# A decoder's 16-head attention, stages three and five: mask by TensorE, sums by a ones column, keys spread by ScalarE, other lags

## What is computed

```
q, k, v = y @ Wq.T, y @ Wk.T, y @ Wv.T          # stage five: q = rope(rmsnorm(y)), k = rope(rmsnorm(ctx)), v = ctx
scores  = q @ k.T / 4, causal mask              # per batch of 64 rows and per head
probs   = softmax(scores)
out     = (probs @ v) @ Wo                      # stage three: only through a modulation of rank 16
m       = 0.1 * tanh(out @ A) * (z @ A2)        # stage three; z is the second norm's input
```

## Time and profile before

| | us |
|---|---|
| median of 3 runs (1977.92 to 2044.46) | 1979.12 |
| the profiled execution | 1981.32 |
| its span, first to last instruction | 1979.4 |
| stage two, from its first transfer to the end | 569 to 705 |
| stage three: statistics, turning, preparation | 705 to 733 |
| stage three: attention | 733 to 915 |
| stage five: statistics, keys | 1476 to 1530 |
| stage five: attention | 1530 to 1676 |
| stage six (feed forward of stage five) | 1676 to the end |

### The profile page before, as it was taken

One profiled execution on the slowest core, in us unless ns is written; L12 is line 12 of the kernel. 1 busy time (PEld: TensorE's weight loads), 2 busy tenths in 40 slices (PEclk: granted clock), 3 DMA queues, 4 the chain that ended last, 5 costly groups with the idle time before them and its releaser, 6 DMA issues. The chain is left out here.

```text
span 1979.4 us, 33807 instructions
## 1 busy us (share of the span) xinstructions
PE 1652.8 (84%) x12770; PEld 1274.6 (64%) x12770; DVE 1253.0 (63%) x2049; ACT 812.3 (41%) x1334; POOL 695.5 (35%) x535
## 2 busy tenths in 40 slices
PE   4999999999948856998997869999960666999997
PEld 3888888888836635776885624444430454788886
DVE  6676777677758878982225869898871897311111
ACT  3555555554526642333223355555520332322222
POOL 0212121212125621001222059999940871232332
PEclk9999999999969968998997879999995698899999
DMA  2011111111030020000001000000019000000001
GB/s 93 14 57 55 63 57 48 56 53 61 24 96 2 3 90 1 2 1 1 1 0 31 5 0 1 1 0 1 0 28 267 1 1 0 1 1 1 1 0 42
DMA packets 59033, 57.45 MB, mean 29 GB/s; under 512 B 17536, under 2 KB 53888, under 8 KB 58928
## 3 DMA queue, kind: packets, MB, share of 16 engines
q1 hardware_dynamic: 58928, 56.00, 9.2%
HBM read 41.31 MB, written 14.68 MB: 28 GB/s over the span
## 5 line engine op out<-in xcount | busy, mean ns | idle before, releaser
L1277 DVE TENSOR_TENSOR s6f_hid<-s6f_act_sb,s6f_u_ps 128x512 f32<-128x512 f32 x64 | 44.0, 687 | 219.1 <-PE s6f_u_ps L1228 219.1
L544 POOL TENSOR_TENSOR s_w_parts<-s_w_raw,s_w_parts 128x768 fp32r<-128x768 f32 x16 | 29.6, 1850 | 429.0 <-ACT s_w_parts L496 429.0
L1300 POOL TENSOR_TENSOR s6f_hid_parts<-s6f_hid,s6f_hid_parts 128x512 fp32r<-128x512 f32 x64 | 82.6, 1291 | 244.3 <-ACT s6f_hid_parts L1266 244.3
L1758 POOL TENSOR_TENSOR s4b_pcs<-s4b_cs,s_p_rows 128x1024 f32<-128x1024 f32 x64 | 120.4, 1903 | 96.6 <-ACT s4b_cs L1804 96.6
L1769 POOL TENSOR_TENSOR s4b_with_re<-s4b_with_re,s4b_with_im 128x1024 f32<-128x1024 f32 x64 | 150.5, 2373 | 2.6 <-DVE s4b_with_im L1723 2.6
L1300 POOL TENSOR_TENSOR s3f_hid_parts<-s3f_hid,s3f_hid_parts 128x512 fp32r<-128x512 f32 x32 | 41.3, 1291 | 265.8 <-ACT s3f_hid_parts L1266 265.8
L1844 PE MATMUL s4b_c_ps<-s4b_pcs,const 128*128 128x512 f32 x256 | 122.5, 601 | 0.0
L420 PE MATMUL s_v_ps<-s_wv_parts,s_xnT 128*128 128x256 f32 x768 | 104.2, 286 | 12.0 <-ACT s_v L525 6.4
L479 PE MATMUL s_o_ps<-s_w_parts,s_zT 128*128 128x256 f32 x768 | 110.4, 294 | 4.1 <-DVE x_rows L583 4.1
L420 PEld LDWEIGHTS s_v_ps<-s_wv_parts,s_xnT 128*128 128x128 f32 x768 | 96.7, 191 | 17.6 <-ACT s_v L525 9.7
L1834 PE MATMUL s4b_turns_ps<-s_theta_bd,s_zc 128*128 128x512 f32 x128 | 78.0, 694 | 31.5 <-DVE s4b_frac L1708 30.4
(11 more groups left out here) (294 smaller groups left out, 4127.3 us busy)
## 6 DMA issues: line engine op xcount, KB each, us to landing
stored_weights<-s1q_halves SPq DMA_DIRECT2D x16, 768.0 KB, 3.7
s6w_parts<-stored_weights SPq DMA_DIRECT2D x32, 384.0 KB, 7.9
s1q_packed<-in_codes SPq DMA_DIRECT2D x8, 384.0 KB, 4.4
s1q_scale<-in_scale_rows SPq DMA_DIRECT2D x8, 384.0 KB, 4.9
x_rows<-in_x SPq DMA_DIRECT2D x1, 2048.0 KB, 8.3
s_w_raw<-in_L_attn_W_Q SPq DMA_DIRECT2D x16, 128.0 KB, 2.2
s_w_raw<-in_L_attn_W_K SPq DMA_DIRECT2D x16, 128.0 KB, 2.3
s_w_raw<-in_L_attn_W_O SPq DMA_DIRECT2D x16, 128.0 KB, 2.4
```

Source lines behind the costliest of these rows:

```text
L1277: nc.vector.tensor_tensor(hid[:, f % 2, :], act_sb[:, f % 2, :], u_ps[:, f % 2, :], ALU.mult) \
L1300: nc.gpsimd.tensor_tensor(hid_parts[:, f % 2, 1, :], hid[:, f % 2, :], hid_parts[:, f % 2, 0, :], ALU.subtract).then_inc(low_done, 1)
L1758: last = nc.gpsimd.tensor_tensor(pcs[:, half, n_, :].rearrange("p (k c) -> p k c", k=HK), cs[:, half, n_, :].rearrange("p (k c) -> p k c", ...
```

## The change

1. The mask is a table of 0 and -1e38, added by TensorE: four float32r products of the identity with it open each tile's scores, and the score products accumulate onto them. The minimum is gone.
2. The values get a 17th column of ones, so that the weighing gives the sums too; the pass over the exponentials is gone. In stage five the spread values of all tiles are made once, on GpSimd, in the keys' block.
3. Keys are spread by ScalarE, with a per-row scale, for two tiles at a time in stage three.
4. Stage three projects q and k from the split halves by float32r products, two tiles at once, q in even steps and k in odd ones; v from both halves by float32. The modulation's factor z @ A2 is made for all tiles in the preparation block. The residual is on GpSimd, all tiles ahead of the low parts. The high parts on ScalarE are done one each in steps 1, 3, 5 and 7.
5. Stage five's queries: ScalarE normalises, GpSimd does four operations with prepared tables; repeated keys are made once in the keys' block.
6. The lags: final and finish 5, `turn_att` 4; all steps are written out. The turned output shares the values' bank.
7. `prefetch` of stage six's weights is issued in the attention's block. The context comes in contiguous layouts made on the host (`ctx_values`, `ctx_rows`).

```diff
-                for half in range(2):
-                    sp.dma_start(vrow[half * S:(half + 1) * S, tiles, :, :].rearrange("k t b d -> k (t b) d"),
-                                 ins["ctx_512"].rearrange("b k d -> k b d")[:, 2 * n * CHUNK:2 * (n + 1) * CHUNK, :]) \
-                        .then_inc(loads[n], 16)
+                sp.dma_start(vrow[:, tiles, :, :].rearrange("p t b d -> p (t b d)"),
+                             ins["ctx_values"][:, 2 * n * CHUNK * S:2 * (n + 1) * CHUNK * S]).then_inc(loads[n], 16)
...
+        va_ps = room.ps("va_ps", [P, 512])
+        v_ps, f_rows, aT_ps = va_ps[:, 0:D], va_ps[:, 0:D], va_ps[:, D:2 * D]
...
-        o_ps, f_ps = of_ps[:, 0:D], of_ps[:, D:2 * D]
-
-        def upto(n):
...
+        def steps(eng, parts):
+            run_steps(eng, NT, parts, head=NT + max(lag for _, lag in parts))
...
+        if prefetch:
+            @block.sync
+            def _(sp):
+                prefetch(sp)
...
+            nc.vector.tensor_copy(ident_r[:, :], core.c("ident")).then_inc(masks, 1)
+            nc.vector.tensor_copy(mask_r[:, :], core.c("mask_add")).then_inc(masks, 1)
...
+            def attended(i, rnd, k):
+                dve.wait_ge(o_full, i + 1)
+                wait(dve, aT_full, i - 1)
+                o = o_ps.rearrange("p (h e) -> p h e", e=EO)
+                nc.vector.reciprocal(rs[:, i % 2, :], o[:, :, E]).then_inc(inverted, 1)
+                dve.wait_ge(inverted, i + 1)
+                nc.vector.tensor_tensor(att[:, i % 2, :].rearrange("p (h e) -> p h e", e=E), o[:, :, 0:E],
+                                        rs[:, i % 2, :].unsqueeze(2).to_broadcast([P, H, E]), ALU.mult) \
+                    .then_inc(att_done, 1)
...
+            def shift(i, rnd, k):
+                scores = s_ps[:, :, 0:4 * S].rearrange("p a (h s) -> p a h s", s=S)
+                dve.wait_ge(s_full, i + 1)
+                nc.vector.tensor_reduce(mx[:, :].rearrange("p (a h) -> p a h", a=4), scores, AX_X, ALU.max) \
+                    .then_inc(maxed, 1)
+                dve.wait_ge(maxed, i + 1)
+                wait(dve, exped, i)
+                nc.vector.tensor_tensor(
+                    sc[:, :, :].rearrange("p (a h) s -> p a h s", a=4), scores,
+                    mx[:, :].rearrange("p (a h) -> p a h", a=4).unsqueeze(3).to_broadcast([P, 4, 4, S]),
+                    ALU.subtract).then_inc(shifted, 1)
...
+                wait(dve, o_full, i - 2)
...
+            steps(dve, [(attended, 4), (shift, 2)] + ([(spread_values, 1)] if own else []) + [(finish, 5)])
...
+                nc.gpsimd.memset(vbd[:, :, :, :, :, :], 0.0).then_inc(zeroed, 1)
+                pool.wait_ge(zeroed, 1)
+                nc.gpsimd.tensor_copy(vbd[:, :, :, :, :, E].rearrange("p k b n h -> p (k b n) h"),
+                                      core.c("half2").unsqueeze(1).to_broadcast([P, 6 * PAIRS, 2])) \
+                    .then_inc(zeroed, 1)
+            def residual(i, rnd, k):
+                nc.gpsimd.tensor_scalar(yt[:, i % 2, :], core.x[:, i, :], mv[:, i, 0:1], rstd[:, i:i + 1],
+                                        ALU.subtract, ALU.mult).then_inc(y_done, 1)
+                pool.wait_ge(y_done, 2 * i + 1)
+                nc.gpsimd.tensor_tensor(core.x[:, i, :], core.x[:, i, :], yt[:, i % 2, :], ALU.add) \
+                    .then_inc(y_done, 1)
...
+            steps(pool, [(residual if own else rope, 0)])
...
+            def normalise(i, rnd, k):
+                wait(act, roped, i - 1)
+                nc.scalar.activation(yt[:, i % 2, :], core.x[:, i, :], ACT.Identity, bias=w["shift"][:, i:i + 1],
+                                     scale=factor[:, i:i + 1]).then_inc(normed, 1)
...
+            def k_copy(n, k, at):
+                rows = qk_ps[:, at:at + NC * AT_ONCE * P].rearrange("p (g s) -> p g s", s=S)
+                for h in range(2):
+                    last = nc.scalar.activation(kbd[:, k, :, :, h, :].rearrange("p c b s -> p (c b) s"), rows,
+                                                ACT.Identity, scale=core.c("blk16")[:, h:h + 1])
+                last.then_inc(k_out, 1)
...
+            def weights(i, rnd, k):
+                if i % 2 == 1 and i // 2 < len(beside[0]):
+                    beside[0][i // 2](act)
+            if own:
+                steps(act, [(probT_copy(0), 3), (tanh, 5), (operands, 0), (probT_copy(1), 3), (attT_copy, 4),
+                            (exponent, 2), (weights, 0)])
+            else:
+                steps(act, [(normalise, 0), (probT_copy(0), 3), (operands, 1), (probT_copy(1), 3), (attT_copy, 4),
+                            (exponent, 2)])
...
+                pair = i // 2
+                if i % 2:
+                    pe.wait_ge(q_out, pair + 1)
+                else:
+                    wait(pe, k_out, pair)
+                wt = w["q_parts"] if i % 2 == 0 else w["k_parts"]
+                for co in range(NC):
+                    for c in range(NC):
+                        for pw, pz in PARTS:
+                            last = nc.tensor.matmul(
+                                qk_ps[:, co * 2 * P:(co + 1) * 2 * P], wt[:, pw, c, co * P:(co + 1) * P],
+                                zT[:, pz, c, 2 * pair:2 * pair + 2, :].rearrange("p t q -> p (t q)"),
+                                start=(c == 0 and (pw, pz) == PARTS[0]),
+                                stop=(c == NC - 1 and (pw, pz) == PARTS[-1]))
+                last.then_inc(qk_full, 1)
...
+                wait(pe, vbd_done, i)
+                wait(pe, aT_out, i - 3)
+                wv = w["wv"].rearrange("p c (n h e) -> p c h n e", h=2, e=E)
+                for b in range(2):
+                    for c in range(NC):
+                        for part in range(2):
+                            for half in range(2):
+                                last = nc.tensor.matmul(
+                                    v_ps[half * S:(half + 1) * S, b * P:(b + 1) * P],
+                                    zT[:, part, c, i, b * S:(b + 1) * S].bitcast(F32), wv[:, c, half, :, :],
+                                    start=(c == 0 and part == 0), stop=(c == NC - 1 and part == 1))
...
+                slot, n = place(i)
+                pe.wait_ge(q_out, i // 2 + 1 if own else i + 1)
+                pe.wait_ge(k_out, i // 2 + 1 if own else i + 1)
+                wait(pe, shifted, i)
                 for j in range(4):
-                    rows = slice(32 * j, 32 * j + 32)
+                    nc.tensor.matmul(s_ps[:, j, 0:4 * S].rearrange("p (h s) -> p h s", s=S), ident_r[:, :],
+                                     mask_r[:, :].unsqueeze(1).to_broadcast([P, 4, S]), start=True, stop=False)
...
+                        for j in range(4):
+                            rows = slice(32 * j, 32 * j + 32)
+                            at = n * P + b * S
                             last = nc.tensor.matmul(
-                                s_ps[b * S:(b + 1) * S, j, at:at + 2 * S], qT[rows, k, c, b * S:(b + 1) * S],
-                                kbd[rows, k, c, b, :, :].rearrange("p h s -> p (h s)"), start=True, stop=True)
+                                s_ps[b * S:(b + 1) * S, j, c * P:(c + 1) * P], qT[rows, slot, c, at:at + S],
+                                kbd[rows, slot, c, n * 2 + b, :, :].rearrange("p h s -> p (h s)"),
+                                start=False, stop=(c == NC - 1))
...
+                            wait(pe, tanhed, i - 1)
+                            pe.wait_ge(vbd_done, i + 1)
...
-                pe.wait_ge(att_done, upto(i + 2))
-                wait(pe, f_out, i)
+                pe.wait_ge(att_done, i + 1)
+                if own:
+                    pe.wait_ge(vbd_done, upto(i + 4))
+                else:
+                    wait(pe, f_out, i)
...
+                    pe.wait_ge(att_done, upto(i + 2))
+                    wait(pe, tanhed, i)
...
+            if own:
+                steps(pe, [(scores, 2), (turn(0), 3), (final, 5), (project_values, 1), (project, 0), (turn(1), 3),
+                           (weigh(0), 3), (turn_att, 4), (weigh(1), 3)])
+            else:
+                steps(pe, [(scores, 2), (turn(0), 3), (final, 5), (turn_qk, 1), (turn(1), 3), (weigh(0), 3),
+                           (turn_att, 4), (weigh(1), 3)])
...
+                pe.wait_ge(a2_low, 1)
+                for g in range(4):
+                    for c in range(NC):
+                        for pw, pz in PARTS:
+                            last = nc.tensor.matmul(m_ps[:, g, :], a2_parts[:, pw, c, :],
+                                                    zT[:, pz, c, g * 4:(g + 1) * 4, :].rearrange("p t q -> p (t q)"),
+                                                    start=(c == 0 and (pw, pz) == PARTS[0]),
+                                                    stop=(c == NC - 1 and (pw, pz) == PARTS[-1]))
...
+                    nc.vector.tensor_copy(
```

(31 more changed lines are left out.)

369 lines of the change are left out of this document (173 added, 196 removed).

## The result

The changed kernel takes 1946.12 us (median of 4 runs, 1944.22 to 1947.61); the kernel before took 1978.63 beside it. The ratio is 0.9836, interval 0.9817 to 0.9856: 32 us less (1.6%, so within the 2% to which the prediction gave 0.04), where 107 were forecast, and outside the range of 1845 to 1905. Its profiled execution has a span of 1942.4 us, 37.0 less than before.

What follows compares the result with a forecast made beforehand. VectorE was taken to bound the loops of stages three and five, TensorE nearly full in stage three. Stage three -37, stage five -62.5 and stage two -7.5 gave -107: 1981.3 to 1874, as median 1872 us, range 1845 to 1905.

Steps and rivals of the forecast that it cites:

- Stage two: Value transfers before stage two's loop: four contiguous for eight strided, so GpSimd waits less for SP; -7.5 us, bounds 5 and 10.
- rival (d): Stages three and five: new waits put a tile's whole chain into each step, 12 us; +156, 2028 us; chance 2%.
- if TensorE's clock in the loops falls below 0.9: Sign that the prediction is wrong: TensorE's granted clock under 0.9 in the loops.
- TensorE, stage three, 7.2 us: TensorE's work per step of stage three's loop: 9.11 - 1.00 - 1.08 - 1.98 + 1.60 + 0.53 = 7.2 us.
- I take nothing: Stage three's value projection, twice the matmuls with half the columns: no added time, between nothing and 1.54 us.
- waits for ScalarE: Stage three's steps: TensorE loses 0.3 us on q tiles, 1.0 on k tiles, 0.6 on average, giving 7.8 us a step.
- The lock in stage three: VectorE's small product at the step's end waits for GpSimd's subtractions: +2 us in all, bounds 0 and 14.
- The start of stage three, -13: From the attention's begin to its first scores: 7 to 8 us remain of 20, so -13 us.
- Stage five: -62.5 forecast: Whole of stage five: -23 us to the first scores, -29 in the loop, -10.5 at the end.
- The keys' chain: Stage five's keys before its attention: start at 1487.5, spread 7.0 to 7.6 us, lock +7, copies 0.8 each; first scores -23 us.
- The ring: Stage five's loop: dependent work from scores to scores sums to 5.55 us, taken as 5.8 a step, bounds 5.0 and 7.0.
- The rule on the lock: VectorE's one-input two-port operations lock against any GpSimd instruction, those with two SBUF inputs only against GpSimd instructions reading SBUF.

Runs made afterwards that it cites:

- e6_low_parts_on_dve: Changed kernel with unread TensorE products at stage two's start, and the three low-part subtractions on VectorE instead of GpSimd: 1877.73 us.
- e9_prefetch_early: Changed kernel with unread TensorE products at stage two's start, and stage six's 32 weight transfers issued again ahead of stage five's keys' block: 1919.51 us.
- e12_fill_only: Changed kernel with unread TensorE products in stage two, three each ahead of the wait of the second and third scores: 1888.72 us.
- e8_no_mask_products: Changed kernel with unread TensorE products at stage two's start, and stage three's four mask products left out: 1880.46 us in one execution.

## Why the prediction was wrong

The direction was right, the time was not. The step that failed is the one under "Stage two": "GpSimd waited 12.0 us for SP ... Off come 10.3, on come four of 0 to 1.29 ... -7.5, bounds 5 and 10". It costed an earlier start at the waiting that it removes and took the 111 us loop behind it as given. The wait did fall, by 6.3 us; the loop grew by 59.5. No rival had it: rival (d) looked for a new wait inside the changed loops, and "if TensorE's clock in the loops falls below 0.9" was said of those alone. Yet the evidence was there: in the trace of the kernel before stage two begins at the low clock and gets the high one 7 us into its loop, and one of three times shown lay 66 us above the others. Add 59.5 + 3.4 + 1.2 (6.3 for 7.5) to the forecast of 1872 and it is 1936, to the measured 1946; the runs with the high clock in stage two (1888) lie in the range and 16 above the forecast. The larger pieces of that rest, in both directions, are the following. That stage five gained more than forecast hides a part of what stage three gained less, and that is luck and not a right sum.

- **TensorE, stage three, 7.2 us: mis-sized.** A slot here is the time from the start of one group of weight loads to the start of the next. In one step of the changed kernel (872.22 to 880.66) they are scores 0.62, turns 0.59 and 0.63, final 0.54, values 1.89, projection 1.44, weighing 0.59 and 0.60, turned output 0.19, mask 0.67: 7.76. The new projection was costed at 1.60 and took 1.44, the mask at 0.53 and took 0.67. "I take nothing" for the value projection was right: its slot was 1.93 before. What was mis-sized is what the sum keeps of the old step as it was, 9.11 - 1.00 - 1.08 - 1.98 = 5.05. The same groups take 5.65 now: the two turns 1.22 for 0.78, the final part 0.54 for 0.34, the weighing 1.19 for 1.08. Why was not tested; in the new order most groups have 0.17 or 0.21 us of "issue" ahead of them. With the 0.17 and 0.69 of waits for ScalarE (0.3 and 1.0 were forecast) the steps are 7.93 and 8.44, mean 8.19 for 7.8: 6 us over 15 steps. First the kernel before, in the step of the earlier trace rows:

```profile
807.55 0.42 PEld L1112 LDWEIGHTS s3a_pT_ps<-const,s3a_ex 128*128 128x128 f32 x4 [0.17 <-ACT s3a_ex L1036]
...
811.85 0.42 PEld L1112 LDWEIGHTS s3a_pT_ps<-const,s3a_ex 128*128 128x128 f32 x4 [0.38 <-issue]
812.24 0.25 PEld L1145 LDWEIGHTS s3a_of_ps<-const,s3a_att 128*128 128x128 f32 x2
...
814.57 0.33 PEld L1153 LDWEIGHTS s3a_of_ps<-s3a_attT,s_WoA 128*16 128x16 f32 x4
```

and the kernel after:

```profile
872.22 0.45 PEld L1113 LDWEIGHTS s3a_s_ps<-s3a_kbd,s3a_qT 32*64 32x64 f32 x32
872.84 0.42 PEld L1125 LDWEIGHTS s3a_pT_ps<-const,s3a_ex 128*128 128x128 f32 x4 [0.17 <-issue]
873.43 0.33 PEld L1170 LDWEIGHTS s3a_of_ps<-s3a_attT,s_WoA 128*16 128x16 f32 x4 [0.17 <-issue]
873.97 1.73 PEld L1082 LDWEIGHTS s3a_va_ps<-s_wv,s_zT 128*64 128x64 f32 x32 [0.21 <-issue]
875.86 1.49 PEld L1066 LDWEIGHTS s3a_qk_ps<-s_zT,s_k_parts 128*128 128x128 f32 x12 [0.17 <-issue]
877.30 0.46 PEld L1125 LDWEIGHTS s3a_pT_ps<-const,s3a_ex 128*128 128x128 f32 x4
877.93 0.55 PEld L1145 LDWEIGHTS s3a_of_ps<-s3a_vbd,s3a_probT 128*64 128x64 f32 x16 [0.17 <-issue]
878.52 0.20 PEld L1159 LDWEIGHTS s3a_va_ps<-const,s3a_att 128*128 128x128 f32 x2
879.40 0.55 PEld L1145 LDWEIGHTS s3a_of_ps<-s3a_vbd,s3a_probT 128*64 128x64 f32 x16 [0.69 <-ACT s3a_probT L1025]
880.00 0.54 PEld L1106 LDWEIGHTS s3a_s_ps<-s3a_mask_r,s3a_ident_r 128*128 128x128 f32 x4
```

- **The lock in stage three, "+2 us in all, bounds 0 and 14": the place was named, the size was wrong.** It is worth 10.2 us (e6_low_parts_on_dve). The product waited through three subtractions and not for the end of one, and the low clock behind the stall came on top.
- **The start of stage three, -13: -9.9.** The chain is as told, but the first projection and values ran in part at 1.2 GHz (granted clock 0.60 and 0.72 in their stretches; 2.57 and 2.61 us for 1.70 and 1.97), where the forecast took warm durations, and the mask's 0.64 us ahead of the first scores was left out. The preparation's +7 came as +6.5.
- **Stage five: -62.5 forecast, -69.1 measured.** The keys' chain as told: start 10.0 us in, spread 8.05 us, lock 4.8 for the forecast 7, copies 0.62 each for 0.8, so -26.3 for -23. The ring is 5.51 us for 5.8, the end 9.1 for 10.5. SP's 36 us were on the path (e9_prefetch_early), and the landing weights cost nothing.
- **The rule on the lock.** VectorE's first product beside the spread, L2018, had begun 0.04 us before it and took its normal 1.22; the next with two SBUF inputs waited, while the sum between them (L2020, one input, 1.22) did not. The Trainium skill, "SBUF — State Buffer", "Who interferes with whom", has both: who issues first keeps the shared ports for its instruction, and an instruction of one SBUF input outside the two-port modes doesn't contend. The trace agrees on both: the spread, begun second, took 8.05 us, and 7.01 in e9_prefetch_early, where it began first.

## What to carry to other kernels

A stage that TensorE doesn't fill at its high clock can be filled by it at its low one, and then can have two lasting speeds (here 3.59 and 5.51 us a unit); its start is part of its cost, and a saving ahead of it (here 6 us) can turn the one into the other (59.5 us). Look for this where the granted clock rises some units into a loop and where single times of a kernel lie one fixed step above the rest; fill the first gap between the units with unread products, placed ahead of a wait that is there anyway, before other changes are measured. And where GpSimd has long operations that read SBUF, look at every VectorE operation with two SBUF inputs that can fall beside them, however small: here one of 0.28 us waited for 11.4.

## What the runs showed of the hardware

- In stage two of the changed kernel TensorE worked at 1.2 GHz for all of the loop's 170.7 us, busy for 160.9 of them, with pauses of 2.73 us between the first two scores and of 0.47 us once a tile. In stage three it stayed at 1.2 GHz through 8.5 us of transposes without a pause (774.8 to 783.3) and rose at some 790.5 us, 3.5 us into the modulation's 24 products of 512 columns. The Trainium skill, "TensorE: Matmul & The Clock Gate", "What's actually happening", says that activity releases the throttle, and that the moment of the change varies between runs with the phase in which the first matmul lands. A phase that varies would fit the toss at equal code (1890 and 1957 us), but no row shows one; that a start 7 us earlier was released in none of 8 executions, and that the loop's work did not release it in 170 us, differs from what the page says, and the measurement decides. Why the earlier start has no chance was not settled; the fill removes the question and does not answer it.
- A VectorE product that waits for the shared ports was not let in between GpSimd's subtractions, which follow each other within 0.1 us: for an operation of 0.28 us, 11.7 us in the changed kernel and in e12_fill_only, 13.1 to 13.3 in six other profiles, and 14.8 in e8_no_mask_products. In the last one it began 1.2 us ahead of the first subtraction (769.60 and 770.84), beside a memset, which only writes, and waited all the same. The addition in the earlier trace rows ran beside a memset in its normal 0.42 us, so whether a write-only operation holds a product of two SBUF inputs is not settled by these rows.
